# Output projection as seven block products, queries computed beside the attention units

## The reference

```
x = x + concat_heads(softmax(mask(q k^T) * scale) v) @ Wo
```

## Time and profile before

| | us |
|---|---|
| median of three runs | 1380.82 |
| the profiled execution | 1379.72 |
| its span, first to last instruction | 1377.9 |
| TensorE busy | 1319.8 |
| VectorE, ScalarE, GpSimd busy | 913.1, 610.7, 552.0 |
| granted clock of TensorE, mean | 0.989 |

### The profile page before, as it was taken

One profiled execution on the slowest core, in us unless ns is written; L12 is line 12 of the kernel. 1 busy time (PEld: TensorE's weight loads), 2 busy tenths in 40 slices (PEclk: granted clock), 3 DMA queues, 4 the chain that ended last, 5 costly groups with the idle time before them and its releaser, 6 DMA issues. The chain is left out here.

```text
span 1377.9 us, 19834 instructions
## 1 busy us (share of the span) xinstructions
PE 1319.8 (96%) x7217; PEld 1131.7 (82%) x7217; DVE 913.1 (66%) x2108; ACT 610.7 (44%) x1236; POOL 552.0 (40%) x290
## 2 busy tenths in 40 slices
PE   5999999999999986999999999999999999988998
PEld 4778888888889986888888888888888888766887
DVE  7788777777776235666666676576666666678653
ACT  3512222122222236566565565556656565156540
POOL 5676776666676643223142241323313232022000
PEclk9999999999999998999999999999999999999999
DMA  7033333232333156112223222222312210300001
GB/s 259 9 130 123 115 115 114 87 111 89 113 115 123 62 195 211 54 41 90 71 85 92 70 84 62 85 69 70 107 39 84 78 61 1 122 3 16 32 32 46
DMA packets 78432, 119.32 MB, mean 87 GB/s; under 512 B 5744, under 2 KB 42608, under 8 KB 78336
## 3 DMA queue, kind: packets, MB, share of 16 engines
q1 hardware_dynamic: 78336, 118.06, 26.0%
HBM read 88.68 MB, written 29.36 MB: 86 GB/s over the span
## 5 line engine op out<-in xcount | busy, mean ns | idle before, releaser
L977 PE MATMUL banks<-xc,wring 128*128 128x512 f32 x1680 | 385.5, 391 | 5.8 <-DVE banks L748 3.3
L977 PEld LDWEIGHTS banks<-xc,wring 128*128 128x128 f32 x1680 | 316.0, 189 | 72.7 <-issue 6.8
L476 POOL TENSOR_TENSOR q_lo<-q_raw,q_hi 128x512 fp32r<-128x512 f32 x64 | 83.0, 1297 | 452.8 <-ACT q_hi L572 452.8
L431 POOL TENSOR_TENSOR wring<-wraw,wring 128x1024 fp32r<-128x1024 f32 x72 | 172.7, 2399 | 120.2 <-ACT wring L553 120.2
L1042 PE MATMUL banks<-wo_hi,oT_hi 128*128 128x512 f32 x512 | 203.5, 398 | 2.5 <-DVE resid L821 2.5
L1042 PE MATMUL banks<-wo_hi,oT_lo 128*128 128x512 f32 x512 | 200.8, 392 | 0.0
L1042 PE MATMUL banks<-wo_lo,oT_hi 128*128 128x512 f32 x512 | 200.6, 392 | 0.0
L553 ACT CAST wring<-wraw 128x1024 fp32r<-128x1024 f32 x72 | 75.7, 1053 | 273.2 <-PE banks L977 116.3
L595 ACT ACTIVATE prob<-prob,shift 128x512 f32<-128x512 f32 (+3 forms) x256 | 140.9, 552 | 34.6 <-DVE shift L792 33.1
L588 ACT CAST pT_hi<-banks 128x512 fp32r<-128x512 f32 (+1 forms) x192 | 86.6, 524 | 149.6 <-PE banks L1018 149.6
L821 DVE TENSOR_TENSOR resid<-banks,resid 128x512 f32<-128x512 f32 x128 | 87.9, 687 | 88.6 <-PE banks L1042 88.4
...
## 6 DMA issues: line engine op xcount, KB each, us to landing
...
```

What stands on the lines that cost most here:

```text
L431: nc.gpsimd.tensor_tensor(wring[:, 1, n % 3, :], factor(s, p), as32(wring[:, 0, n % 3, :]), ALU.subtract).then_inc(w_lo, 1)
L476: nc.gpsimd.tensor_tensor(qh[1][:, u % 3, :], q_raw[:, u % 3, :], as32(qh[0][:, u % 3, :]), ALU.subtract).then_inc(q_lo, 1)
L977: ins = nc.tensor.matmul(dst, wring[:, a, n % 3, k * 256 + fb * P:k * 256 + (fb + 1) * P], xc[:, XI[p], c, k, :], start=first, stop=(k == ...
```

## The change

Only five panels are projected ahead of the units: keys, the first group's queries, values. The queries of the other groups are computed beside the units from 14 narrow panels of 256 columns, seven jobs each (98 jobs, 12 matmuls of 512 columns), one or two in each unit from 1 to 52. The last half products of the value panel run in units 0 and 1. The jobs write two banks in turn; ScalarE keeps P1, VectorE reads the others (`read_job`), GpSimd adds the two turned halves (`turn_added`), rounds the low parts and forms the sums of the weight quarters.

The outputs of the heads are no longer kept on chip. ScalarE copies each (with negative sign for the second batch) from the mixed bank, SP stores it to HBM, for early heads of the first batch four times; GpSimd adds further copies up with accumulating transfers from HBM to HBM, which gives the sums for seven block products of the output. The first of these is computed in two halves as 16 first steps of 12 matmuls (15 in units 56 to 63, one behind them). The other six follow as 48 steps of 24 matmuls, for which Wo lies in SBUF whole; its sums are made by VectorE (`wt`), and the context is rounded in the last 16 steps.

In each unit the order of TensorE is scores, first filler, second filler, mixing of the unit before, transposes. `turn_probs(u)` waits for ScalarE's copy of the output. SP loads queries two units ahead, in rings of two. Wo comes in three bursts: w00 (4.2 MB) in unit 51, w10, w11 and half of w01 (10.5 MB) behind the last job, the rest (2.1 MB) with x (4.2 MB) and two context tiles behind the last unit. A_w and B_w (4.2 MB) come ahead of step 33's factors. The diff is cut to this core; "..." marks what is left out.

```diff
-PANELS = 12
...
+NARROW = 14
+JOBS = 7 * NARROW
+PLACES = ([(1, 1)] + [(u, p) for u in range(2, 34) for p in (0, 1)]
+          + [(u, p) for u in range(34, UNITS) for p in (0, 1) if p == 0 or u % 4 != 1])
+JOB_AT = {pl: j for j, pl in enumerate(PLACES[:JOBS])}
+JOB_UNIT = [u for u, p in PLACES[:JOBS]]
...
+PAIRS = 8
+FIRST_STEPS = 2 * PAIRS
+REST = [(u, p) for u in range(LAST_JOB_UNIT + 2, UNITS) for p in (0, 1)]
+STEP_AT = {pl: n for n, pl in enumerate(REST[len(REST) - FIRST_STEPS + 1:])}
+O_STORES = {(0, 0): ("A00", "S2", "S3", "S4"), (1, 0): ("S1",), (0, 1): ("A01",), (1, 1): ("N11",)}
...
+        def keep_out(u):
+            sp.wait_ge(o_copied, u + 1)
+            for name in o_names(u):
+                sp.dma_start(o_dram[name][o_place(u)[1]], o_st[u % 2][:]).then_inc(o_kept[u % 2], 16)
...
+        def load_wo(part, head, half, arrived):
+            k0 = head * HEAD
+            n = part.shape[1]
+            for c in range(0, n, 4):
+                sp.dma_start(part[:, c:c + 4, :],
+                             Wo[k0 + c * HEAD:k0 + (c + 4) * HEAD, half * 512:half * 512 + 512]
+                             .rearrange("(k p) c -> p k c", p=P)).then_inc(arrived, 16)
...
+            if u + 2 < UNITS:
+                load_q(u + 2)
...
+            if (u - 1, 0) in JOB_AT:
+                keep_turned(JOB_AT[u - 1, 0])
...
+                keep_turned(JOB_AT[u - 1, 1])
+            if u == JOB_UNIT[7 * (NARROW - 1) + 3] + 1:
+                sp.wait_ge(job_done, 7 * (NARROW - 1) + 3)
+                load_wo(w00, 0, 0, w00_in)
+            if u == LAST_JOB_UNIT + 1:
+                sp.wait_ge(job_done, JOBS)
+                load_wo(w10, 2 * PAIRS, 0, w10_in)
+                load_wo(w11, 2 * PAIRS, 1, w11_in)
+                load_wo(w01[0], 0, 1, w01_in[0])
+            if u >= LAST_JOB_UNIT + 1 and u + 2 < UNITS:
+                for f in steps_of(u + 2):
+                    load_first(f)
+        keep_out(UNITS - 2)
+        load_first(FIRST_STEPS - 1)
+        load_step(0)
+        load_step(1)
+        keep_out(UNITS - 1)
+        sp.wait_ge(mix_done, UNITS)
+        load_wo(w01[1], PAIRS, 1, w01_in[1])
         for t in range(TT):
             sp.dma_start(resid[:, t, :], x_t[t]).then_inc(x_in[t], 16)
-        for u in range(UNITS):
-            if u + 3 < UNITS:
-                load_q(u + 3)
-            if u % 4 == 0 and half_of(u) + 1 < HALVES:
-                load_kv(half_of(u) + 1)
-            for m in wo_after(u):
-                if m + 2 < 4 * GROUPS:
-                    load_wo(m + 2)
-            if u % 4 == 2 and half_of(u) + 1 < HALVES:
...
+        def accumulate(name, source, g, before):
+            k = 4 * (g % 4)
+            if before:
+                pool.wait_ge(s_added[name], 16 * before)
+            nc.gpsimd.dma_start(out=o_dram[name][k:k + 4].rearrange("k p c -> (k p) c"),
+                                in_=o_dram[source][k:k + 4].rearrange("k p c -> (k p) c"),
+                                accum_op=ALU.add, max_dma_last_dim=8192).then_inc(s_added[name], 16)
...
-        pool.wait_ge(p_done, done(PANELS - 1, "P4", 1))
...
+                turn_added(JOB_AT[u - 1, 0])
...
-                wo_low(m)
+            for j in jobs_of(u + 1):
+                narrow_sums(j)
+                narrow_low(j)
+            if (u - 1, 1) in JOB_AT:
+                turn_added(JOB_AT[u - 1, 1])
+            for f in steps_of(u + 1):
+                first_low(f)
+            if u % 8 == 2 and u >= 8:
+                accumulate_negated(u // 8 - 1)
+            if u % 8 == 6 and u >= 32:
+                accumulate_plain(u // 8)
+        first_low(FIRST_STEPS - 1)
+        accumulate_negated(GROUPS - 1)
...
+            else:
+                act.wait_ge(job_done, j - 3)
+            if p in ("P1", "P2", "P4"):
...
+        def first_high(f):
+            q = f % PAIRS
+            act.wait_ge(o_in[f % 2], 16 * (f // 2 + 1))
+            if f == 0:
+                act.wait_ge(job_done, JOBS)
+                act.wait_ge(turn_made, 4 * NARROW)
+            if f >= 2:
+                act.wait_ge(first_done, f - 1)
+            nc.scalar.copy(oa[0][:, f % 2, :, 0:256], oraw[:, f % 2, :, 0:256]).then_inc(fa_hi, 1)
+            act.wait_ge(w00_in, 16 * 4)
+            nc.scalar.copy(ob[0][:, f % 2, :, :], w00[:, 2 * q:2 * q + 2, :]).then_inc(fb_hi, 1)
+        def keep_first(f):
+            if f % PAIRS == PAIRS - 1:
+                act.wait_ge(first_done, f + 1)
+                for n in range(2):
+                    nc.scalar.copy(p1[:, 2 * (f // PAIRS) + n, :], banks[:, 6 + n, :]).then_inc(first_read, 1)
...
-        def out_high(u):
+        def keep_out(u):
             act.wait_ge(mix_done, u + 1)
-            if half_of(u) >= 2:
-                act.wait_ge(piece_done, 8 * (half_of(u) - 1))
-            nc.scalar.copy(oT[0][:, half_of(u) % 2, u % 4, :], mixed[:]).then_inc(o_hi, 1)
+            if u >= 2:
+                act.wait_ge(o_kept[u % 2], o_count(u - 2))
+            nc.scalar.activation(o_st[u % 2][:], mixed[:], ACT.Identity,
+                                 scale=-1.0 if batch_of(u) else 1.0).then_inc(o_copied, 1)
...
-            for m in wo_after(u):
-                wo_high(m)
+            for j in jobs_of(u + 1):
+                narrow_high(j)
+            if (u + 1, 0) in STEP_AT:
+                first_high(STEP_AT[u + 1, 0])
             exps(u)
             normalise_wide(u)
+            if (u, 0) in JOB_AT:
+                keep_job(JOB_AT[u, 0])
+            if (u, 0) in STEP_AT:
+                keep_first(STEP_AT[u, 0])
+            if (u + 1, 1) in STEP_AT:
+                first_high(STEP_AT[u + 1, 1])
             if u > 0:
-                out_high(u - 1)
-            if u % 4 == 1:
-                scale_ctx(half_of(u))
+                keep_out(u - 1)
         probs_high(UNITS - 1)
-        out_high(UNITS - 1)
+        first_high(FIRST_STEPS - 1)
...
+        def job_turn(b, n):
+            if n >= 1:
+                dve.wait_ge(turn_made, n)
+            nc.vector.tensor_tensor(n_turn[0:64, 0, :], b[64:128, :], sin[64:128, :], ALU.mult)
+            nc.vector.tensor_tensor(n_turn[64:128, 0, :], b[0:64, :], sin[0:64, :], ALU.mult)
+            nc.vector.tensor_tensor(n_turn[:, 1, :], b, cos[:], ALU.mult).then_inc(job_read, 1)
+        def read_job(j):
+            e, p, b = j // 7, SEQ[j % 7], job_bank(j)
+            if p == "P1":
+                return
+            dve.wait_ge(job_done, j + 1)
+            dve.wait_ge(job_p1, e + 1)
+            if p == "P6":
+                nc.vector.tensor_tensor(n_u[:, 0, :], b, n_p1[:], ALU.add).then_inc(job_read, 1)
+            elif p == "P7":
+                nc.vector.tensor_tensor(n_u[:, 1, :], b, n_p1[:], ALU.add).then_inc(job_read, 1)
+            elif p == "P2":
+                job_turn(b, 4 * e + TURNS[p])
+            elif p == "P5":
+                dve.wait_ge(job_read, 6 * e + 3)
+                nc.vector.tensor_tensor(n_u[:, 0, :], b, n_u[:, 0, :], ALU.add)
+                link(nc.vector.tensor_tensor(b, b, n_u[:, 1, :], ALU.add))
+                job_turn(b, 4 * e + TURNS[p])
+            elif p == "P4":
+                link(nc.vector.tensor_tensor(b, b, n_p1[:], ALU.add))
+                job_turn(b, 4 * e + TURNS[p])
+            else:
+                dve.wait_ge(job_read, 6 * e + 4)
+                link(nc.vector.tensor_tensor(b, b, n_u[:, 0, :], ALU.add))
+                job_turn(b, 4 * e + TURNS[p])
...
+        def read_banks(m):
+            p = OUT[m]
+            dve.wait_ge(step_done, PAIRS * (m + 1))
...
+                if u == 1:
+                    dve.wait_ge(st[0], 16 * (TILES - 8) // 4)
+                    dve.wait_ge(st[1], 16 * (TILES - 8) // 4)
                 probs_low(u - 1)
             peaks(u)
+            if u == 0:
+                c11(LASTP, 1)
+            if u == 1:
+                c01(LASTP, 1)
+            if (u - 1, 1) in JOB_AT:
+                read_job(JOB_AT[u - 1, 1])
             normalise(u)
-            for n in pieces_of(u)[:1]:
-                add_piece(n)
...
-            for n in pieces_of(u)[1:]:
-                add_piece(n)
-            if u % 4 == 1:
-                quant_ctx(half_of(u))
...
+                read_job(JOB_AT[u, 0])
         probs_low(UNITS - 1)
-        add_piece(PIECES - 10)
-        out_low(UNITS - 1)
-        add_piece(PIECES - 9)
-        dve.wait_ge(added, PIECES - 8)
-        for t in range(TPB):
+        for s in range(STEPS):
+            m, q = s // PAIRS, s % PAIRS
+            step_low(s)
+            if m < 4:
+                wt(m, q)
+            else:
+                quant_ctx(s - 4 * PAIRS)
+            if m >= 1 and q == 1:
+                read_banks(m - 1)
+            if m >= 1 and q == 2:
+                add_copies(m - 1)
+            if m == 5 and 3 <= q < 3 + TPB:
+                row_stats(nc, resid, stats, moments, q - 3, link)
```

(60 more changed lines are left out.)

665 lines of the change are left out of this document (468 added, 197 removed).

## The result

The changed kernel takes **1545.3 us** (median of 4 runs, 1544.4 to 1548.5) against 1381.1 beside it: ratio 1.120, 95% interval 1.118 to 1.122. It is slower, as forecast, by 164 us and not by 109, and lies above the forecast's range of 1425 to 1530. The profiled execution has a span of 1542.4 us. Of all executions of all kernels one stood far off in the slow state (3954.8 us, in the run that moves only the wait for the copy); no ratio holds it.

A forecast was written before the change was run, and what follows sets the result against it. The kernel was taken to be bound by TensorE's number of matmuls. Savings of -64.3 us and added waits summed to +109.5 us on 1379.7, giving 1489 us, range 1425 to 1530.

The forecast's parts named there:

- The copy that the new order uncovers: In two-filler and some one-filler units, transposes wait for ScalarE's copy of the mixed bank, now uncovered: 52 x 0.9 = +46.8 us.
- Fewer matmuls: Output product on TensorE: 1344 matmuls in place of 1536, queries cost the same; -43.7 us.
- the first five units: Units without filler before: value panel's last half products and jobs now fill TensorE's idle time there; -20.6 us.
- units 57 to 59: Units 57 to 63: ScalarE's rounding of factors delays exponentials and copy, a unit lasts 12.4 us; +17.6 us, bounds 5 and 25.
- The reads of the second filler's bank: Second job of a unit waits until VectorE, behind the peaks, has read its bank; +34.9 us, bounds 10 and 50.
- GpSimd and ScalarE in these units: Where P6 comes next, ScalarE waits for three sums ahead of its exponentials, mostly covered by other waits; +2 us, bounds 0 to 10.
- The accumulating transfers: GpSimd's 28 HBM-to-HBM transfers of 1 MB stay hidden beside the units; 0 us, up to +40 if ahead of loads.
- The third rival: Accumulates, stores and narrow weight loads make every load late, ScalarE waits for queries in many units; 1529 us, 16%.
- The first burst: Unit 55's queries wait behind 10.5 MB of Wo for 17.6 us, then the clock is lower; +20.2 us, bounds 8 and 32.
- Behind the units: Step 2's factors wait behind 7.3 MB of loads, 15.3 us plus 2.66 of clock: +17.9 us; the last first step adds +5.4.
- The end: Behind the last step, VectorE's bank reads, sums and statistics take 13.3 us before the next stage; +10.7 us with the clock.
- The filler places hide their waits: Rival: units stay at 10.46 us and the matmul count decides; 1405 us, or 1359 with harmless bursts; 10%.

## Why the prediction was right, and where it was wrong

The direction and most of the terms were right; 1489 was 55 us too low, because two costs had been put at nothing: the accumulating transfers, and the clock behind the short waits in the units.

- **The copy that the new order uncovers**, 52 x 0.9: right in mechanism and size. The row says 0.78 of idle time, and putting the mixing back takes the unit from 11.30 to 10.40.
- **Fewer matmuls; the first five units; units 57 to 59**: right. A unit with first steps lasts 12.5 us for 12.4, and unit 60's start of the next group was the exception (21.2 for 16.4, through late operands and the lower clock).
- **The reads of the second filler's bank**, +34.9: right in mechanism, and 39.3 in size. The waits are 0.86 behind a read of P2 (0.8 predicted), 2.08 behind P5 (2.15), 1.8 behind P4 and 1.1 to 2.2 behind P3 (1.55 both). The condition for the upper bound, GpSimd's sums holding n_turn, was not met: VectorE never waits for GpSimd's addition here.
- **The clock behind these waits**: a step that failed, by having no term. The prediction charged the lower clock behind the bursts (2.66 us each) and nothing behind the waits of 0.8 to 2.2 us that it foresaw in the units. It is **17.6 us** with the 0.3 that goes with each such unit. It comes behind some waits and not behind others of the same length (units 8 and 40); why was not tested.
- **GpSimd and ScalarE in these units**, "taken +2", bounds 0 to 10: 4.6 in the changed kernel. That the waits above already cover the late exponentials was right there: making the sums earlier and out of VectorE's way gained nothing (1545.1). It holds only in that order. With the mixing put back the reads are early, and then late sums are what the long units wait for: moved to GpSimd's idle 4.6 us, they gave 36 us. The prediction counted GpSimd's 26 us of work in 42, and not that the work starts late, behind a wait for the turned tile (4.63 us in unit 8), nor that it can hold VectorE's normalising (18 us, lost and won back with one wait).
- **The accumulating transfers**, taken 0 ("hidden"), bounds 0 to +40: the largest step that failed. Without them the time is **24 us** less: 15 at step 2, 6 in unit 53 and 6 in unit 55, less what units 56 to 59 give back. They are hidden beside ordinary units, as the prediction had it (units 2 to 51 last 615.6 us with them and 614.9 without), and not where a burst of loads already runs. The third rival had the mechanism, transfers and loads in each other's way, but foresaw late queries in many units.
- **The first burst**, +20.2: mis-sized. Unit 55's wait of 27.4 us falls into 21.3 of the burst and 6 of the transfers. The 3.7 us left over 17.6 fit the row of SP's queue, which issues the queries only at 912.13, not right behind the burst's issue; that part is read from the trace and was not tried by itself.
- **Behind the units**, step 2: 15.3 predicted, 15.96 without the accumulating transfers, 30.7 with them. Mis-sized because they were left out, not because the bytes were.
- **The last first step** (7.1 for 5.4) and **A_w and B_w** (a wait of 6.6 for 5.8) came out near their sizes. **The end** was +8.2, not +10.7: from the column sums (1357.22) to the next stage (1371.07) 13.85 us, 5.66 before.

Units 2 to 51 are 24.5 us over (61.4 against 36.9), which is 4.4 of reads, 2.6 of late probabilities and 17.6 without a wait. The misses sum to 24.5 + 14.8 (units 52 to 56, 73.9 against 8.6 + 3 x 7.1 + 9.0 + 20.2) + 7.9 (units 57 to 62, 86.3 against 6 x 12.4 + 4) + 15.4 = 63 us; the error is 55. The other terms together lay some 8 us below their prices: 2.5 is the end and 2.8 the 11.30 us of 46 units where 11.36 were predicted; the rest is open. Two slips in the prediction's readings change no term: the units 5 to 62 end at 1158.70, so that one lasts 10.48 us on the mean and not 10.46, and a tile with one sum ahead takes 2.9 us in the rows, which its 6.32 uses, not 2.84.

*The filler places hide their waits*, the rival on the other side, was wrong as told: nothing hid them. The design does reach that side, by 0.5%, once order, sums, loads and transfers are each given their own place.
